# A down product in seven block products instead of eight, in a fused layer-norm, projection and gated feed-forward kernel

## The reference

```python
h = _layernorm(x) * (1 + ca) + sa
x = x + ga * (h @ (weight * block_mask).T + bias)
h = _layernorm(x) * (1 + cb) + sb
gate = h @ (gate_w * gate_s).T          # weights are int32 in -128..127, a scale for each row
up = h @ (up_w * up_s).T
x = x + gb * ((silu(gate) * up) @ (down_w * down_s).T)
```

## Time and profile before

| | us |
|---|---|
| median of 3 executions | 1166.69 (1166.21 to 1168.19) |
| the profiled execution | 1165.9 |
| its span, first to last instruction | 1164.1 |
| PE busy in it | 1126.4 (97%), 4789 matmuls |
| DVE busy | 650.3 (56%) |
| ACT busy | 395.7 (34%) |
| POOL busy | 340.9 (29%) |
| granted TensorE clock, mean | 0.990 |
| DMA | 167.10 MB, mean 144 GB/s |

### The profile page before, as it was taken

One profiled execution on the slowest core, in us unless ns is written; L12 is line 12 of the kernel. 1 busy time (PEld: TensorE's weight loads), 2 busy tenths in 40 slices (PEclk: granted clock), 3 DMA queues, 4 the chain that ended last, 5 costly groups with the idle time before them and its releaser, 6 DMA issues.

```text
span 1164.1 us, 13047 instructions
## 1 busy us (share of the span) xinstructions
PE 1126.4 (97%) x4789; PEld 529.6 (45%) x4789; DVE 650.3 (56%) x829; ACT 395.7 (34%) x715; POOL 340.9 (29%) x348
## 2 busy tenths in 40 slices
PE   5989999999999989999999999999999999999998
PEld 3544544545444434444444444444444444444444
DVE  4879957766675776867666666564432222222222
ACT  0322036656463444544544545443330000000000
POOL 1133327457644433434443334331110000000000
PEclk9989899999999999999999999999999999999999
DMA  9993221335344356655555556421744433434320
GB/s 346 401 341 86 73 70 40 108 91 172 135 163 127 94 132 186 175 136 137 148 148 138 147 140 150 109 64 37 271 154 153 148 136 128 151 113 151 103 103 37
DMA packets 88736, 167.10 MB, mean 144 GB/s; under 512 B 18592, under 2 KB 53152, under 8 KB 85984
## 3 DMA queue, kind: packets, MB, share of 16 engines
q1 hardware_dynamic: 77168, 125.88, 34.5%
q0 software_dynamic: 11504, 40.38, 11.7%
HBM read 117.47 MB, written 48.76 MB: 143 GB/s over the span
## 4 chain that ended last, share of the span: by engine, by line
PE 78%; DVE 9%; DMA 4%; SPq 3%; issue 2%; ACT 2%; POOL 1%; DVEq 1%; POOLq 0%; ACTq 0%
PE pA L1108 26%; PE pA L977 13%; PE pA L1204 12%; PE pB L1108 12%; PE pB L1204 12%; DVE work L1321 3%; DMA work<-in_L_wmod 2%; PE pB L966 2%; DMA work<-in_L_ffn_up_w 1%; DVE work L1484 1%; SPq L461 1%; ACT work L757 1%; SPq L482 1%; SPq L451 1%; DVE work L1319 1%
## 5 line engine op out<-in xcount | busy, mean ns | idle before, releaser
L1108 PE MATMUL pA<-work 128*128 128x512 f16 x1680 | 380.0, 381 | 7.8 <-ACT work L877 4.5
L1108 PEld LDWEIGHTS pA<-work 128*128 128x128 f16 x1680 | 164.7, 98 | 209.1 <-ACT work L877 6.4
L977 PE MATMUL pA<-work 128*128 128x512 f32 x512 | 229.5, 604 | 2.8 <-ACT work L779 1.1
L1108 PE MATMUL pB<-work 128*128 128x512 f16 x752 | 176.8, 380 | 1.5 <-DVE work L1484 1.5
L977 PEld LDWEIGHTS pA<-work 128*128 128x128 f32 x512 | 97.3, 194 | 118.1 <-issue 114.7
L1204 PE MATMUL pA<-work 128*128 128x512 f16 x672 | 147.6, 379 | 0.0
L700 POOL DMA_DIRECT2D h_scratch<-work x84 | 64.4, 766 | 276.7 <-DVE work L1498 276.5
L877 ACT ACTIVATE work<-pA 128x512 f32<-128x512 f32 x126 | 75.0, 595 | 188.2 <-PE pA L1108 188.0
L1204 PE MATMUL pB<-work 128*128 128x512 f16 x630 | 138.4, 379 | 0.0
L1498 DVE SCALAR_TENSOR_TENSOR work<-work 128x512 f16<-128x512 f16 x84 | 69.5, 828 | 104.1 <-ACT work L883 104.1
L757 ACT ACTIVATE work<-pB,small 128x128 f32<-128x128 f32 x256 | 92.3, 477 | 84.2 <-PE pB L966 77.7
(11 more groups left out here) (134 smaller groups left out, 937.2 us busy)
## 6 DMA issues: line engine op xcount, KB each, us to landing
work<-h_scratch SPq DMA_DIRECT2D x16, 1376.0 KB, 6.0
h_scratch<-work POOLq DMA_DIRECT2D x84, 256.0 KB, 3.3
work<-in_L_wmod SPq DMA_DIRECT2D x10, 2048.0 KB, 17.7
work<-in_L_ffn_gate_w SPq DMA_DIRECT2D x84, 128.0 KB, 3.7
work<-in_L_ffn_up_w SPq DMA_DIRECT2D x84, 128.0 KB, 3.7
work<-in_L_ffn_down_w SPq DMA_DIRECT2D x96, 112.0 KB, 2.6
work<-in_L_attn_data SPq DMA_DIRECT2D x16, 512.0 KB, 4.4
x_scratch<-work POOLq DMA_DIRECT2D x16, 512.0 KB, 5.6
```

The costliest lines, as they stand in the source:

```text
L977: last = pe.matmul(pA[:, 2 * par(t) + h, :], hT1[par(t)][:, c, :], wT[:, c, h * H:(h + 1) * H], start=(c == 0), stop=(c == KT - 1))
L1108: last = pe.matmul(ps, w[:, m, c], bc[b][:, mv_, s, c], start=begin, stop=(i == n - 1 and c == KT // 2 - 1 and s == 1), skip_group_check=True)
```

## The change

The down product is also made by seven block products. A pair of token tiles is one row of blocks, a pair of chunks (2i, 2i+1) one column; ten pairs, and chunk 20 and the tail are left over and multiplied as before, three matmuls for each tile and half. For each pair of tiles:

- P1 = A11 W11 and P6 = S2 WT2 and P7 = S3 WT3 add up in banks 6 and 7 (high and low part); P2 = A12 W21 and later P4 = A22 WT4 in banks 0 and 1; P5 = S1 WT1 and P3 = S4 W22 in banks 2 and 3. P1 is read by ACT and DVE into a snapshot, so are P6 and P7. The order is 1, 2, 6, 5, 7, 4, 3, each of 20 matmuls with 512 columns.
- The A side now has seven combinations of h2, which are made in gate and up, on fp32 values: A11 and S3 behind an even chunk, A12, A22, S1, S2 and S4 behind an odd one, with A12 and A22 alone behind chunk 20. S3 is a subtraction on DVE; S1, S2 and S4 are sums on POOL (`odd_sums`). Each output gets a high part (ACT), a low part (DVE) and has its place in one of four single buffers, where h2 had two by turns. The product of an even chunk is kept in `keep[b]` until the odd one.
- The weight side has seven combinations too. Four are cast by ACT from two units, three new and one rewritten by POOL (`combine_down`), once for both units. There are 25 down units, one in each of the groups 14 to 38, with 8, 8 and 5 chunks for each. The load is split in seven of 1.31 MB and one of 0.79 MB for the leftovers.
- In gate and up snap1 and snap3 share a buffer, so snap1 of a group waits for both additions of up of the group before; the addition of up[1] waits for the first of the three sums of an odd group before, that of up[0] for the third.
- The units of gate and up are transposed ahead of the second low part, not behind it. The slices for gb start at group 3 instead of 4. The last `sums` of the layer norm stand before the stores of group 0 in POOL's order. The second tail is before group 40, not 41. Some semaphores are joined, and one power of two is 12 instead of 14.

Cut to its core:

```diff
-        TAIL_BEFORE = {GROUPS.index((FT - SK, 1)): 0, NG - 1: 1}
+        TAIL_BEFORE = {GROUPS.index((FT - SK, 1)): 0, NG - 2: 1}
...
+        OUTS = {"even": (A11, S3), "odd": (A12, A22, S1, S2, S4), "plain": (A12, A22)}
...
# SP, between gate and up and down
+            wait_h2_stored(0)
             load_h2(0)
+            sp.wait_ge(down_stored, 16 * down_stores(NDN))
+            for m in (W11, W21, WT2):
+                load_wd(m)
+            sp.wait_ge(tail_ready, 4)
+            load_wd(WT1)
+            sp.wait_ge(s4_stored, 16 * stores_before(NG, S4))
+            sp.dma_start(wl.rearrange("p c k d -> p (c k d)"), wl_d.rearrange("p c k d -> p (c k d)")).then_inc(wl_loaded, 16)
             sp.wait_ge(p3_done, NG)
+            for m in (WT3, WT4, W22):
+                load_wd(m)
...
# POOL
+            def odd_sums(g):
+                b, n, before = GROUPS[g][1], 3 * groups_before(g, "odd"), partner(g)
+                pool.wait_ge(h2_lo, outs_until(before, S3))
+                pool.wait_ge(prod2_ready, g + 1)
+                pool.tensor_tensor(keep[b][1], keep[b][1], up[1], ALU.add).then_inc(s_ready, 1)
+                pool.wait_ge(s_ready, n + 1)
+                pool.tensor_tensor(keep[b][0], keep[b][1], keep[b][0], ALU.subtract).then_inc(s_ready, 1)
+                pool.wait_ge(s_ready, n + 2)
+                pool.tensor_tensor(gate[1], up[0], keep[b][0], ALU.subtract).then_inc(s_ready, 1)
...
+            def combine_down(u):
...
+                pool.tensor_tensor(w[:, WT1], w[:, WT3], w[:, W11], ALU.subtract).then_inc(down_combined, 1)
+                pool.wait_ge(down_combined, n + 1)
+                pool.tensor_tensor(w[:, WT3], w[:, W22], w[:, WT3], ALU.subtract).then_inc(down_combined, 1)
+                pool.tensor_tensor(w[:, WT2], w[:, W22], w[:, WT1], ALU.subtract).then_inc(down_combined, 1)
+                pool.wait_ge(down_combined, n + 3)
+                pool.tensor_tensor(w[:, WT4], w[:, W21], w[:, WT2], ALU.subtract).then_inc(down_combined, 1)
...
+                if g == 1:
+                    sums(LAST)
+                if g:
+                    kind = kind_of(g - 1)
+                    if kind == "odd":
+                        odd_sums(g - 1)
+                    store_outs(g - 1, A11 if kind == "even" else A12)
+                    for u in turned_in[g - 1]:
+                        if UNITS[u][0] == "dnl" or UNITS[u][0] == "dn" and UNITS[u][1] >= 4:
+                            combine_down(u)
+                    if kind == "odd":
+                        store_outs(g - 1, S1)
+                        store_outs(g - 1, S4)
                 if g < NG:
                     for u in turned_in[g]:
                         if UNITS[u][0] == "gu" and UNITS[u][2] == 1:
                             pair_sums(UNITS[u][1])
...
# ACT, in each group
-                        act.wait_ge(gate1_ready, g)
+                        act.wait_ge(up1_ready, g)
+                        act.wait_ge(up2_ready, g)
                     take(snap1, run_bank[k]).then_inc(snap1_ready, 1)
...
                     take(snap3, run_bank[k]).then_inc(snap3_ready, 1)
...
+                for m in outs[2:]:
+                    hi_of(g - 1, m)
...
# PE
+            for q in range(NQ):
...
+                pe.wait_ge(h2_loaded[q % 2], 32 * (q // 2 + 1))
+                down_product(q, drun, A11, W11)
+                if q == 0:
...
+                    pe.wait_ge(wl_loaded, 16)
+                else:
+                    pe.wait_ge(read_out, 4 * q - 1)
+                down_product(q, done_, A12, W21, left=(0, 0))
...
+                pe.wait_ge(dsnap_ready, 3 * q + 1)
+                down_product(q, drun, S2, WT2, first=False)
...
# DVE
+            def wait_read(g, half):
+
+                if kind_of(g - 1) == "even":
+                    dve.wait_ge((prod1_ready, prod2_ready)[half], g)
+                    return
+                dve.wait_ge(h2_lo, outs_until(g - 1, (A12, A22)[half]))
+                if kind_of(g - 1) == "odd":
+                    dve.wait_ge(s_ready, 3 * groups_before(g - 1, "odd") + (3, 1)[half])
...
+                        wait_read(g, 1)
                     hi_plus(up[1], five_bank[k], snap3).then_inc(up2_ready, 1)
```

More of the change, by code:

```diff
@@ L47, in adaln_kernel @@
     A11, A12, S3, A22, S1, S2, S4 = range(NC)
+    NPR = FT // 2
+    ORDER = [A11, S3, A12, A22, S1, S2, S4]
+    W11, W21, WT3, W22, WT1, WT2, WT4 = range(NC)
+    F_FROM = [0, 8, 16]
+    F_SIZE = [8, 8, 5]
     x_v = data.rearrange("o (n p) d -> (o n) p d", p=P)
@@ L268, in adaln_kernel @@
         mask_bits = sem("mask_bits")
[L269 removed]
+        masked_by_dve, masked_by_pool = sem("masked_by_dve"), sem("masked_by_pool")
         w_turned = sem("w_turned")
@@ L389, in adaln_kernel, with down_stores, kind_of, outs_until @@
         TAIL_UNIT = [k[0] for k in UNITS].index("tail")
+        def down_stores(n):
+            return sum(0 if kind == "dn" and d < 4 else 2 if f == 2 else 1 for kind, d, f in DOWN[:n])
+        OUTS = {"even": (A11, S3), "odd": (A12, A22, S1, S2, S4), "plain": (A12, A22)}
+        STORES = {A11: (out_even, even_stored), A12: (out_a, a_stored), S1: (out_s12, s12_stored), S4: (out_s4, s4_stored)}
+        HOME = {A11: A11, S3: A11, A12: A12, A22: A12, S1: S1, S2: S1, S4: S4}
+        def kind_of(g):
+            c = GROUPS[g][0]
+            return "plain" if c == FT - 1 else ("even", "odd")[c % 2]
+        def outs_until(g, m):
+            return sum(len(OUTS[kind_of(i)]) for i in range(g)) + OUTS[kind_of(g)].index(m) + 1
+        def stores_before(g, home, blk=None):
+            return sum(1 + (kind_of(i) == "plain") for i in range(g)
+                       if home in OUTS[kind_of(i)] and blk in (None, GROUPS[i][1]))
+        def groups_before(g, kind):
+            return sum(1 for i in range(g) if kind_of(i) == kind)
+        def partner(g):
+            c, b = GROUPS[g]
+            return GROUPS.index((c - 1, b))
+        def value_of(g, m):
+            b = GROUPS[g][1]
+            if m in (S3, S4):
+                return gate[1]
+            if m == A11:
+                return keep[b][0]
+            if m in (S1, S2):
+                return keep[b][m == S1]
+            return up[m == A22]
         MID = {3: 0, 6: 1, 7: 3, 8: 5, 9: 6, **{t: t - 2 for t in range(10, NT + 1)}}
@@ L542, in stored_groups @@
[L542 to L550 removed]
+            last_of_blk = [GROUPS.index((FT - 1, b)) for b in range(2)]
@@ L1539, in _ @@
                     times(g - 1, 1)
-                    lo_of(g - 1, 1)
+                    if kind == "even":
+                        b = GROUPS[g - 1][1]
+                        dve.wait_ge(prod1_ready, g)
+                        dve.wait_ge(prod2_ready, g)
+                        dve.tensor_tensor(gate[1], keep[b][0], keep[b][1], ALU.subtract).then_inc(s3_ready, 1)
+                if g and g < NG:
+                    for u in turned_in[g]:
+                        if u not in dn_index:
+                            turn_unit(u)
+                if g:
+                    lo_of(g - 1, outs[1])
                 if g < NG:
                     for u in turned_in[g]:
-                        if u not in dn_index and g:
+                        if u in dn_index:
                             turn_unit(u)
```

583 lines of the change are left out of this document (368 added, 215 removed).

## The result

The kernel after takes **1205.35 us** (median of 4 runs, 1202.90 to 1214.26), the kernel before 1166.64 us beside it: ratio 1.0338 [1.0315, 1.0361]. It is slower by 3.4%, where 1157.3 us, 0.8% faster, was forecast. The profiled execution took 1207.13 us with a span of 1205.3, against 1165.9 and 1164.1.

What follows compares the result with a forecast made beforehand. PE was taken as the bound, with hardly a gap from the sixteenth group on. Terms -34.5 - 3.9 + 15.5 + 7 + 6.5 = -9.4 on 1165.9 gave 1156.5, plus 0.8 for the median: 1157.3 us; 8-in-10 range 1141 to 1177.

Steps and rivals of the forecast that it cites:

- Steady groups, by hand: Gate and up from group 18: POOL's queue makes PE wait for the odd sums in five odd pairs, +15.5 us.
- Work added to gate and up: Odd groups get three more high parts, low parts and POOL sums; every second group from 17 four 1.15 us down sums.
- The steady term of +15.5: PE waits at groups 19, 23, 31 and 35 (3.3 us each) and 27 (2.3); ends 0 and 34.
- The exclusion of DVE and POOL: DVE operations with two SBUF inputs and POOL sums wait for each other's whole instruction; low parts near 1.1 us, not 0.83.
- busy over 70% of groups 17 to 36: Sign for the forecast: POOL busy over 70% between groups 17 and 36 of gate and up.
- First groups: Early gate and up: last layer norm sums ahead of the h2 store, -3.9 us; earlier gb slices, +7 (0 to 14).
- the slices start a group earlier: Gate and up groups 4 to 6 and 9: units queue on SP behind the gb slices, +7 us (0 to 14).
- signs of being wrong: Forecast wrong if POOL's odd sums start by T+11 of the second odd group, or PE also waits in groups 8 to 16.
- Down: Down product: 160 fewer matmuls, -34.5 us; P3 and next pairs' loads at 0; stage 262.4 us plus one DMA wait.
- The leftover wait: Start of down: leftover weights load only after the last S4 store; 4.8 and 1.7 for clock, +6.5 us (2 to 10).
- The slower one: Rival: eight odd pairs from group 6 run at DVE and POOL's pace, 40 instead of 15.5, 1181.8 us; chance 0.2.
- The queue has room: Rival: POOL's sums of group 19 start before the 23.0 PE allows, so +15.5 is gone, 1141.8 us; chance 0.2.

Runs made afterwards that it cites:

- cast late: Kernel after, with ACT casting a pair's first down unit behind snap3 and the high parts, and DVE transposing down units at the group's end: 1177.87 us.
- no down sums: Kernel after, with POOL's sums of the down weights in `combine_down` left out and the store kept: 1157.50 us.
- pair sums later: Kernel after with the down cast moved late and POOL's four gate and up weight sums moved behind the odd sums: 1160.53 us.
- four changes of order and buffers: Kernel after with down cast late, gate and up weight sums later, a second tail output buffer, and leftover weights loaded early: 1147.73 us.

## Why the prediction was wrong

**The step that failed** is in "Steady groups, by hand". It followed POOL's queue ("four down sums ... done 18.1; store 19.1") to the sums behind the store, and not the store itself to the one who waits for it. The wait had been in the code in front of me: one buffer, casts that wait until it is stored, and the cast ahead of silu and snap2 in ACT's order. The forecast's own times, from the start T of an odd group behind an odd one, were enough. In them the store is issued at T+18.1, and with the 3.3 us of a store of h2 it lands at T+21.4. The next group starts at T+12.1 and wants snap2 behind five products, at T+20.7; the cast, silu and snapshot take 2.2 us from the landing, so PE would go on at T+23.6, 2.9 us late. In the kernel after, group 19 is such a group and starts at 580.6. Its chain that ended last, the four sums from T+11.9, the store from T+18.1, and P7 of group 20 at T+25.3:

```profile
592.53 1.18 POOL work L843
...
598.68 5.12 DMA down_scratch<-work
...
605.86 8.77 PE pA L1286 x32
```

So POOL's queue was foreseen to some 0.3 us. What was missing is the step behind it: the landing took 5.12 us, and PE waited 4.37. In "Work added to gate and up" the sums and the store stood only as time on POOL. Cost: 47.0 us. That the store wait is its cause is shown from two sides: with the cast moved out from ahead of the snapshot the eleven waits are gone (cast late), and with the store issued 5 us earlier 1.4 us of them are left (no down sums).

**The steady term of +15.5** was worked out rightly for a kernel that wasn't this one. In the kernel after none of its waits can be seen; once the cast is late they are there, 16.7 us in fourteen waits, in five pairs and in none of those without down sums. That the total came out so near is partly luck: the waits in the places that were named came to 12.0 us, and 4.8 fell on snap2 instead, behind DVE's additions. (The upper end of 34 is a slip as well: twice 15.5 is 31.) In the kernel after the longer wait hides this one. So the term to put in the sum was 47 in place of 15.5, not both.

**The exclusion of DVE and POOL** The earlier trace rows holds: L1739, the low part, has a mean of 894 ns where it was 828 before, with a median of 692 and a maximum of 1835, and DVE's additions from PSUM, L1717, are at 685 and 681. I had said near 1.1 us, which is too much, also for the kernel without the store waits (987 ns, pair sums later). POOL was said to be busy over 70% of groups 17 to 36; in the second stretch of the table above it was 194.23 of 309.80 us, 63%, since the waits had made the groups longer; without them it is the 74% given above. The row of the low part in the kernel before, by form:

```profile
L1498 DVE SCALAR_TENSOR_TENSOR work<-work 128x512 f16<-128x512 f16 x84 | 69.5, 828 | 104.1 <-ACT work L883 104.1
```

**The second tail** (10.7 us) is in no term. The diff moved it to before group 40, and "the diff moves a tail" was not followed to what its single output buffer waits for: a small store. That store was issued at 893.70, 5.4 us after SP had issued the load of the first h2 of down, 4480 KB, whose median is 13.7 us; it landed at 904.59. POOL itself had issued a store of 448 KB at 889.49, which took 13.4 us to land. That the load, and not this store ahead of it, caused the delay is argued from these times, not tried; that the single buffer turns it into a wait of PE is shown.

**First groups**: -3.9 + 7 = +3.1 was forecast, +7.0 measured. The order of `sums` is worth 2.2 alone, not 3.9: two later waits, hidden before, came up. If that holds inside the change too, the rest, +7 by the slices, came to about 9. But "the slices start a group earlier" can't be all of it: starting them later again gave 2.5 us by the rows and nothing that the medians show. POOL's pair sums ahead of the odd sums are another part, which the forecast did not have here: moved, they gave 2.4 us (with the cast late) and 3.5 us (alone) by the rows of these groups. Where the rest of the 9 us comes from stays open. One of the forecast's own signs of being wrong, that PE also waits in groups 8 to 16, is there too: four waits of 0.59 to 1.91 us in groups 9, 10 and 14.

**Down** was right in each of its terms. Without the wait for the leftovers, 269.2 - 6.7 = 262.5 us, where 297.1 - 34.5 = 262.6 was forecast: the seven products keep their beat (260.00 us with PE busy in 259.99), neither P3 nor h2 of a next pair is late. The leftover wait was put at 4.8 and 1.7 for the clock. The timeline of PE of the kernel after:

```profile
941.11 6.16 PE L1353 MATMUL pA<-work 128*128 128x512 f16 x20 [4.87 <-DMA work<-down_left_scratch]
```

4.87 of idle time, 1.68 for the clock (20 matmuls are shown as 6.16 us where the undisturbed 20 are shown as 4.48) and 0.16 as at each wait: 6.7, where 6.5 was forecast.

**The sum again**, with what was measured: 1.1 ahead of gate and up, 7.0 + 47.0 + 10.7 + 2.3 in it, -34.6 + 6.7 for down, 1.0 at the end: +41.2 on 1165.9.

**The rivals.** The slower one had the right sign at 1181.8 and the wrong mechanism: its point was DVE's addition of up. It had 0.2; the store wait had no chance of its own, and the measured time lies above the whole range. "The queue has room" is nearly what the version with the pair sums moved shows behind group 16 (4.8 us in place of 16.7): there was room, but only in another order. (Where the forecast calls the case in which the steady term is 0 "the second rival", it means this one, the first of its list.) The rule on the shared port (the Trainium skill, page "SBUF — State Buffer", section "SBUF: two separate sides"), that such a DVE operation and a POOL operation shut each other out, agreed with the trace, as L1739's maximum of 1835 ns beside its median of 692 shows, and was not what decided.

## What to carry to other kernels

For every semaphore of a buffer that a change makes bigger or fills later, follow the chain to its end: who refills it, where does that instruction stand in its engine's order, and who is queued behind it. A buffer that is combined and stored as a whole is free later than one stored piece by piece, and an in-order engine should meet that wait only behind what the bottleneck needs. A wait can hide another, so edits are judged together: moving the pair sums gave 0.9 us alone and 17.3 behind the late cast. The seven-product down pays 34.6 us in its own stage; with four changes of order and buffers 19 us of it, 1.7% of the kernel, are left.

## What the runs showed of the hardware

After a wait of 2.08 us 32 matmuls took 8.77 us instead of 7.08, after one of 2.50 in the same kernel 7.08; at the same places in the kernel with two tail buffers 2.51 was followed by 8.67, and 3.88 by 9.90 where 3.83 had been followed by 8.77. So the length of the wait alone doesn't say what the clock does behind it. The granted clock (the last but two of the columns) at the start of three such stretches of the kernel after, behind the waits of 3.83, 1.44 and 2.50 us:

```profile
575.50:579.00 3.50, 3.50 (x10) 1.28 (x11) 3.40 (x5) 1.70 (x4) 0.41 (x1) 0.59 0.05 7
633.30:636.80 3.50, 3.47 (x17) 1.59 (x18) 3.40 (x5) 2.75 (x4) 0.33 (x1) 1.00 0.02 4
...
690.40:693.90 3.50, 3.50 (x17) 1.61 (x18) 3.40 (x6) 2.69 (x4) 0.39 (x1) 1.00 0.04 9
```

0.59 means that most of these 3.5 us ran at the lower of the two levels, 1.2 GHz, and 1.00 is 2.4 GHz. With two tail buffers the same stretch behind 2.51 us was at 0.53. Adding 1.7 us to each wait over 2 us, as the forecast did, gives 8 x 1.7 = 13.6 for the eleven, where 12.7 was measured, but 4.9 us more with the same waits in another kernel.

A store of 128 KB, issued at 893.70, took 10.89 us to land, with a load of 4480 KB and a store of 448 KB under way; the median of the four such stores is 4.5 us.
